# A new order of the small work around a 16-head attention tile: one head swapped between VectorE and GpSimd, two rows read from SBUF, casts and sums at other places

## The chip, the cores and the metric

One core of a Trainium2 chip. The metric is the device time of the whole program in microseconds. Engines are named TensorE (PE in the rows), VectorE (DVE), ScalarE (ACT), GpSimd (POOL) and SyncE (SP, which here only issues DMAs).

## The reference

Four layers on an input of 8 sequences of 1024 tokens with 256 channels, in float32: attention, a linear layer with fp8 rounding, a state-space mixer with its MLP, and a gated MLP, each with a layer norm ahead and a residual. The change touches the attention alone:

```python
q = (x @ Wq.T + bq).reshape(b, s, 16, 16)          # x is the layer norm of the input
attn_scores = einsum('bihd,bjhd->bhij', q, k) / 4
logits = li[:, :, None, :] + lj[:, None, :, :] + rel_b      # li, lj: three numbers per token
relation_probs = softmax(logits, axis=-1)                   # b, i, j, 3
bias = einsum('bijk,hk->bhij', relation_probs, logical_bias)
attn_scores = attn_scores + gate * bias                     # gate: sigmoid, per head and query
out = einsum('bhij,bjhd->bihd', softmax(attn_scores), v)
```

For each query i and key j there is thus a softmax over three relations, shared by all 16 heads, and each head adds its own mixture of it to its scores.

## The kernel before

The attention stage goes over 64 tiles of 128 queries, 8 tiles per sequence (called a batch here). For a tile there are two smooth terms, `R[k][0]` and `R[k][1]` (128 queries x 1024 keys, float32, in SBUF; k is the parity of the tile). Each head h does, in this order:

* f(h): `row = R1 * rho[h] + R0`. VectorE does it in one instruction (`dve_f`, L306), reading R1 from a copy in PSUM, `ps_p`, which ScalarE makes once a tile (`act_p`, L357). For the heads of `POOL_HEADS` GpSimd does it in two (`pool_f`, L224 and L226), from SBUF. Rows go through 8 buffers.
* TensorE computes the scores of head h into `ps_s` (`pe_s`, L465). There is one such buffer, so that of h+1 waits for s(h).
* s(h): VectorE adds the scores and the row, with a minimum along the keys (`dve_s`, L317).
* e(h): ScalarE takes the exponential (`act_e`, L394). Two heads later TensorE transposes (`pe_t`, L476), and ScalarE copies the two halves back (`act_at`, L403); TensorE then multiplies by V (L488).

While the heads of tile t run, four more jobs are done between them, at places written out by hand: `body` of each engine has a loop over u = 0..15 with lines such as `if look and u == 8: act_y0(act, t + 1)`; GpSimd's `body` is a plain list. Nothing is planned at run time: each engine goes through its own list in order, and semaphores make it wait.

1. The smooth terms of tile t+1. VectorE: two maxima into RT (`dve_rel`, L289 and L292, at u = 0 and 1). GpSimd: two subtractions (`pool_rel`, L199). ScalarE: three exponentials (`act_rel`, L377 and L381). GpSimd: two sums (`pool_sum`, L204 and L207). ScalarE: `act_y0`, an Ln (L387) and an Exp (L389). GpSimd: a product (`pool_t`, L211). VectorE: `dve_y` (L297, at u = 11, behind s(11)). GpSimd: two products (`pool_p`, L216), which end R0 and R1. They read a small tile `cur` (gate and two offsets per query), which ScalarE copies from `small` (`act_cur`, L352).
2. The projections of tile t+9: layer norm (`dve_ln` L248 at u = 2, `pool_rstd` L185, `dve_xn` L256 at u = 5), transposes and products on TensorE (`pe_xT`, `pe_d`, `pe_g`, `pe_qk_proj`), `act_d` (L340, L343), a clamp on GpSimd (`pool_gT`, L230), and q and k into `qkf` (`dve_qk`, L263 and L265, behind s(15)).
3. The splitting of that `qkf` into three bfloat16 parts, one tile later: `act_hi` (L362), `pool_rem` (L189), `act_mid` (L366), `pool_lo` (L193). The SP queue then writes the parts to HBM (`sp_parts`, L527), and reads them back as Q (L544, once a tile) and K (L536, once a batch, 24 DMAs in four groups; each group waits until the one before has landed and until the heads that use it are done in the last tile of the old batch). The order of this queue at a batch's end is: parts of the last tile of the next batch, 24 key loads, the loop's branch, the load of `xt` for the next layer norm (L522).
4. The output of tile t-1: `dve_norm`, `dve_out`, `act_o`, `act_aT`, `pool_xrb` (L243), and TensorE's transposes and product.

## Time and profile before

| | us |
|---|---|
| median of 3 runs | 6644.66 (6643.51 to 6645.17) |
| the profiled execution: its own time | 6645.17 |
| the profiled execution: its span | 6643.4 |
| attention stage, first to last tile | about 186 to 3153 |
| DVE busy in the span | 4750.4 (72%) |
| ACT busy | 4472.4 (67%) |
| PE busy | 5605.6 (84%) |
| POOL busy | 3670.1 (55%) |

The busy shares are means over stages of different kinds and cover the three later layers too. In the attention stage all four engines are busy most of the time and hand rows to each other head by head, so that a share alone doesn't say who waits. The order in time of one tile, engine by engine, does.

### The profile page before, as it was taken

What the parts mean: (1) busy time and instruction counts of PE and PEld (TensorE: products, weight loads), DVE (VectorE), ACT (ScalarE), POOL (GpSimd) and SP (SyncE); (2) the same over time, 40 slices, a digit from 0 to 9 for tenths busy, and PEclk for the clock granted to TensorE, in tenths of its full rate; (3) what the DMA queues carried; (4) which work ended last, traced back from release to release, by engine and by line L of the source; (5) the groups of instructions that cost most, each with busy time, mean ns of one, the idle gap of its engine ahead of it and who ended that gap; (6) DMA issues with size and microseconds to landing.
All of it is one profiled execution on the core that took longest, in us unless ns stands there. A gap on an engine that the chain in (4) does not pass through costs nothing. (4 is left out here: it accounts for less than half of the span.)

```text
span 6643.4 us, 125291 instructions
## 1 busy us (share of the span) xinstructions
PE 5605.6 (84%) x40354; PEld 3636.9 (55%) x40354; DVE 4750.4 (72%) x6130; ACT 4472.4 (67%) x7170; POOL 3670.1 (55%) x2047
## 2 busy tenths in 40 slices
PE   4688888888888888888436989889989988999999
PEld 3466666666565656655323444444444445666665
DVE  1788888888888888888776988888888792122121
ACT  1798989989898989999214778788787781111111
POOL 2777777777777777777122765675576580000000
PEclk7899999999999999999767989999999999999999
DMA  1212121111212121120222232232232222111110
GB/s 32 45 26 47 26 46 26 34 39 27 46 26 46 27 46 29 27 39 14 68 99 91 105 111 95 97 120 96 104 108 100 93 99 94 47 32 32 47 32 10
DMA packets 374621, 386.46 MB, mean 58 GB/s; under 512 B 223392, under 2 KB 300960, under 8 KB 374064
## 3 DMA queue, kind: packets, MB, share of 16 engines
q1 hardware_dynamic: 374064, 379.00, 19.8%
q8 instruction: 353, 5.78, 0.4%
q14 instruction: 204, 1.67, 0.1%
HBM read 293.58 MB, written 85.33 MB: 57 GB/s over the span
## 5 line engine op out<-in xcount | busy, mean ns | idle before, releaser
L317 DVE CUSTOM_DVE_ANT_0 srow<-srow,ps_s,cur 128x1024 f32<-128x1024 f32 x1024 | 1303.7, 1273 | 263.8 <-PE ps_s L465 183.0
L394 ACT ACTIVATE srow<-srow,nmax 128x1024 f32<-128x1024 f32 x1024 | 1190.9, 1163 | 207.8 <-DVE nmax L317 194.7
L403 ACT COPY AT<-ps_t 128x512 f32<-128x512 f32 x2048 | 1106.4, 597 | 73.5 <-PE ps_t L476 66.1
L1520 POOL TENSOR_TENSOR c_hc<-c_hs,c_cs 128x1024 f32<-128x1024 f32 x384 | 923.2, 2424 | 365.4 <-PE c_ps_y L1473 219.4
L476 PEld LDWEIGHTS ps_t<-ident,srow 128*128 128x128 f32 x8192 | 964.8, 143 | 279.7 <-ACT AT L403 84.8
L476 PE MATMUL ps_t<-ident,srow 128*128 128x128 f32 x8192 | 1106.0, 279 | 12.6 <-ACT AT L403 8.3
L1473 PE MATMUL c_ps_y<-c_hc,c_ident 128*128 128x512 f32 x2048 | 1009.0, 621 | 62.7 <-POOL c_hc L1520 61.9
L465 PE MATMUL ps_s<-K,Q 96*128 96x512 bf16 x2048 | 633.3, 391 | 436.9 <-DVE nmax L317 331.6
L306 DVE SCALAR_TENSOR_TENSOR srow<-ps_p,rho,R 128x1024 f32<-128x1024 f32 x768 | 975.0, 1270 | 13.7 <-ACT ps_p L357 9.2
L1784 DVE TENSOR_TENSOR_SCAN c_hs<-c_da,c_pd 128x1024 f32<-128x1024 f32 x384 | 868.6, 2279 | 151.7 <-PE c_pd L1459 128.4
L1570 ACT ACTIVATE c_sT<-c_room,c_bT 128x256 f32<-128x256 f32 x1536 | 647.8, 493 | 1.4
L226 POOL TENSOR_TENSOR srow<-srow,R 128x1024 f32<-128x1024 f32 x256 | 610.2, 2384 | 47.0 <-POOL srow L224 47.0
L488 PE MATMUL ps_o<-AT,V 128*32 128x128 f32 x16384 | 621.2, 281 | 1.6 <-issue 1.6
L1473 PEld LDWEIGHTS c_ps_y<-c_hc,c_ident 128*128 128x128 f32 x2048 | 367.0, 197 | 405.9 <-issue 288.5
L1459 PEld LDWEIGHTS c_pd<-c_ident,c_sT 128*128 128x128 f32 x3072 | 369.6, 147 | 319.7 <-issue 223.7
L1937 POOL TENSOR_TENSOR d_rstd<-d_ve,d_mhalf 128x4 f32<-128x4 f32 x16 | 16.3, 1019 | 898.6 <-DVE d_ve L969 898.6
L1512 POOL TENSOR_TENSOR c_db<-c_conv,c_bs 128x1024 f32<-128x1024 f32 x128 | 317.3, 2485 | 326.4 <-DMA c_bs<-bc_rows_d 225.2
L465 PEld LDWEIGHTS ps_s<-K,Q 96*128 96x128 bf16 x2048 | 133.4, 98 | 656.7 <-DVE nmax L317 542.7
L1561 ACT ACTIVATE c_da<-c_dt,c_a_neg 128x1024 f32<-128x1024 f32 x384 | 436.7, 1140 | 78.0 <-DVE c_hs L1784 77.7
L1459 PE MATMUL c_pd<-c_ident,c_sT 128*128 128x128 f32 x3072 | 422.2, 283 | 76.5 <-ACT c_sT L1570 60.9
L488 PEld LDWEIGHTS ps_o<-AT,V 128*32 128x32 f32 x16384 | 409.0, 111 | 137.3 <-issue 133.9
L199 POOL TENSOR_TENSOR R<-Dj,RT 128x1024 f32<-128x1024 f32 x128 | 300.8, 2372 | 301.9 <-DVE RT L292 301.9
(200 smaller groups left out, 8567.4 us busy)
## 6 DMA issues: line engine op xcount, KB each, us to landing
c_cs<-bc_rows_d SPq DMA_DIRECT2D x256, 512.0 KB, 3.8
c_bs<-bc_rows_d SPq DMA_DIRECT2D x64, 512.0 KB, 4.7
parts_d<-parts SPq DMA_DIRECT2D x65, 384.0 KB, 3.3
K<-parts_d SPq DMA_DIRECT2D x192, 128.0 KB, 4.5
Q<-parts_d SPq DMA_DIRECT2D x384, 64.0 KB, 2.9
ym_d<-c_conv SPq DMA_DIRECT2D x32, 512.0 KB, 2.6
d_ym<-ym_d SPq DMA_DIRECT2D x16, 1024.0 KB, 7.2
xt<-in_x SPq DMA_DIRECT2D x65, 128.0 KB, 3.3
```

The lines of the kernel that those rows point to most:

```text
L306: nc.vector.scalar_tensor_tensor(r[:], ps_p[:], rho[:, h:h + 1], R[k][0][:], ALU.mult, ALU.add).then_inc(fd_ok, 1)
L317: nc.vector.tensor_tensor_reduce(r[:], r[:], ps_s[:], cur[k][:, h:h + 1], BIG, ALU.add, ALU.min, nmax[:, h % NROW:h % NROW + 1]).then_inc( ...
L394: nc.scalar.activation(r[:], r[:], ACT.Exp, scale=-1.0, bias=nmax[:, h % NROW:h % NROW + 1]).then_inc(e_ok, 1)
L403: nc.scalar.copy(AT[h % NAT][:, HG * half:HG * half + HG, :], ps_t[:, half]).then_inc(at_ok, 1)
L465: last = nc.tensor.matmul(ps_s[:, n * 512:(n + 1) * 512], Q6[k][:, h, :], K6[:, h, n * 512:(n + 1) * 512], start=True, stop=True)
L476: last = nc.tensor.transpose(ps_t[:, half, i, :], rows_sb[h % NROW][:, j * P:(j + 1) * P], ident[:])
L488: last = nc.tensor.matmul(ps_o[32 * i:32 * i + 32, j, :], V[par][:, n, h, :], AT[h % NAT][:, n, :], start=(n == 0), stop=(n == NT - 1))
L1459: last = nc.tensor.transpose(pd[:, c, k * P:(k + 1) * P], src[:, k, c * P:(c + 1) * P], ident[:])
L1473: last = nc.tensor.matmul(ps_y[:, c, cut], ident[:], hc[(2 * n + c) % RING][:, cut], start=n == 0, stop=n == NS - 1)
L1520: nc.gpsimd.tensor_tensor(hc[(2 * n + c) % RING][:], hs[(2 * ROWS_T.index(n) + c) % NHS][:], cs[n % RING][:], ALU.mult).then_inc(hp_ok, 1)
L1570: last = nc.scalar.activation(sT[i % NSC][:, k, :], dtxT[:, k, pair * PD:(pair + 1) * PD], ACT.Copy, scale=bT[:, k, n:n + 1])
L1784: nc.vector.tensor_tensor_scan(hs[j % NHS][:], da[c][:], pd[:, c, :], 0.0, ALU.mult, ALU.add).then_inc(h_ok, 1)
```

## The change

* `POOL_HEADS` goes from (1, 4, 8, 12) to (4, 8, 12, 15). GpSimd no longer makes row 1 of the next tile ahead; it makes row 15 of the tile itself, behind the clamp.
* VectorE makes rows 0 and 1 from `R[k][1]` in SBUF in place of `ps_p` (`FROM_PSUM = 2`). Row 0 of the next tile comes ahead of s(15), row 1 behind it.
* The copy into `cur` goes from ScalarE to VectorE, ahead of L289, as a `tensor_scalar` with a wait for its own end.
* GpSimd's list: the remainder L189 comes ahead of the two subtractions, L193 ahead of f(8) and the sums.
* ScalarE's list: the second and third exponentials at u = 4 and 5 (they were at 3 and 4), L366 at 3 (4), `act_y0` at 9 (8), `act_d` at 11 (12), the copy into `ps_p` at 15 (14).
* TensorE's list: `pe_g` at u = 10 (11), `pe_qk_proj` at 12 and 13 (13 and 14).

```diff
--- before.py
+++ after.py
@@ -52,9 +52,10 @@
 
     AHEAD = NT + 1
     NROW = 8
-    POOL_HEADS = (1, 4, 8, 12)
+    POOL_HEADS = (4, 8, 12, 15)
     DVE_HEADS = tuple(h for h in range(H) if h not in POOL_HEADS)
     NPH, NDH = len(POOL_HEADS), len(DVE_HEADS)
+    FROM_PSUM = 2
     LAG = 2
     TINY, HUGE = 1e-15, 1e15
     NAT = 2 * HG
@@ -283,8 +284,13 @@
             d10, d20 = (Dj[:, i:i + 1, bass.ds(((t // NT) % 2) * S, S)].rearrange("p a s -> p (a s)") for i in range(2))
             a10, a20 = (cur[k][:, H + i:H + i + 1] for i in range(2))
             if step == 0:
-                wait(dve, cur_ok, t + 1)
+                wait(dve, kap_ok, t + 1)
+                wait(dve, a12_ok, t + 1)
                 wait(dve, p_ok, 2 * t)
+                wait(dve, s_ok, H * (t - 1))
+                nc.vector.tensor_scalar(cur[k][:].unsqueeze(1), small[:, bass.ds(t % (2 * NT), 1), :],
+                                        1.0, None, ALU.mult).then_inc(cur_ok, 1)
+                dve.wait_ge(cur_ok, t + 1)
                 wait(dve, pm_free, 4 * (NT * (t // NT) + NT) - 1)
                 nc.vector.tensor_scalar(RT[:], d10, a10, 0.0, ALU.add, ALU.max).then_inc(rel_step, 1)
             elif step == 1:
@@ -301,9 +307,12 @@
                 return
             r = rows_sb[h % NROW]
             if h == 0:
+                wait(dve, p_ok, 2 * t + 2)
+            elif h == FROM_PSUM:
                 wait(dve, pc_ok, t + 1)
+            p1 = R[k][1] if h < FROM_PSUM else ps_p
             wait(dve, t_ok, 2 * (H * t + h) + 2)
-            nc.vector.scalar_tensor_tensor(r[:], ps_p[:], rho[:, h:h + 1], R[k][0][:],
+            nc.vector.scalar_tensor_tensor(r[:], p1[:], rho[:, h:h + 1], R[k][0][:],
                                            ALU.mult, ALU.add).then_inc(fd_ok, 1)
 
         def dve_s(dve, t, k, h):
@@ -345,11 +354,6 @@
             last.then_inc(eT_ok, 1)
             act.wait_ge(eT_ok, p + 1)
             act.sem_inc(pm_free, 1)
-
-        def act_cur(act, t, k):
-            wait(act, kap_ok, t + 1)
-            wait(act, a12_ok, t + 1)
-            nc.scalar.copy(cur[k][:].unsqueeze(1), small[:, bass.ds(t % (2 * NT), 1), :]).then_inc(cur_ok, 1)
 
         def act_p(act, t, k):
             wait(act, p_ok, 2 * t + 2)
@@ -668,21 +672,20 @@
                 pool_t(pool, 0)
                 pool_p(pool, 0, 0, 0)
                 pool_p(pool, 0, 0, 1)
-                pool_f(pool, 0, 0, 1)
 
             def body(pool, t, k, par, ib, pro, post, look, before):
                 pool_f(pool, t, k, 4)
+                if followed(t, pro):
+                    pool_rem(pool, t - 1 + AHEAD)
                 for n in range(2 * look):
                     pool_rel(pool, t + 1, 1 - k, n)
                 if pro:
                     pool_rstd(pool, t + AHEAD)
                 if followed(t, pro):
-                    pool_rem(pool, t - 1 + AHEAD)
+                    pool_lo(pool, t - 1 + AHEAD)
                 pool_f(pool, t, k, 8)
                 for n in range(2 * look):
                     pool_sum(pool, t + 1, 1 - k, n)
-                if followed(t, pro):
-                    pool_lo(pool, t - 1 + AHEAD)
                 if post:
                     pool_xrb(pool, t - 1)
                 pool_f(pool, t, k, 12)
@@ -694,8 +697,7 @@
                     pool_p(pool, t + 1, 1 - k, n)
                 if pro:
                     pool_gT(pool, t + AHEAD)
-                if look:
-                    pool_f(pool, t + 1, 1 - k, 1)
+                pool_f(pool, t, k, 15)
                 if pro:
                     pool_kappa(pool, t + NT, 1 - par, ib)
 
@@ -732,6 +734,8 @@
                 for u in range(H):
                     if u + 1 < H:
                         dve_f(dve, t, k, u + 1)
+                    elif look:
+                        dve_f(dve, t + 1, 1 - k, 0)
                     dve_s(dve, t, k, u)
                     if look and u < 2:
                         dve_rel(dve, t + 1, 1 - k, u)
@@ -751,8 +755,6 @@
                         dve_gate(dve, t + NT)
                     if pro and u == 15:
                         dve_qk(dve, t + AHEAD)
-                    if look and u == 15:
-                        dve_f(dve, t + 1, 1 - k, 0)
 
             def finish(dve):
                 dve_out(dve, TILES - 2)
@@ -824,8 +826,6 @@
 
             def start(act):
                 front(act, NT)
-                for t in range(2):
-                    act_cur(act, t, t)
                 for step in range(3):
                     act_rel(act, 0, 0, step)
                 act_y0(act, 0)
@@ -842,9 +842,9 @@
                         act_hi(act, t - 1 + AHEAD)
                     if u == 0 and (not isinstance(t, int) or t >= 2):
                         act_aT(act, t - 2)
-                    if look and u in (1, 3, 4):
-                        act_rel(act, t + 1, 1 - k, (1, 3, 4).index(u))
-                    if followed(t, pro) and u == 4:
+                    if look and u in (1, 4, 5):
+                        act_rel(act, t + 1, 1 - k, (1, 4, 5).index(u))
+                    if followed(t, pro) and u == 3:
                         act_mid(act, t - 1 + AHEAD)
                     if post and u == 5:
                         act_o(act, t - 1)
@@ -852,14 +852,12 @@
                         act_gate(act, t + NT, 1 - par, ib)
                     if pro and u == 8:
                         act_xT(act, t + AHEAD)
-                    if look and u == 8:
+                    if look and u == 9:
                         act_y0(act, t + 1)
-                    if pro and u == 12:
+                    if pro and u == 11:
                         act_d(act, t + AHEAD)
-                    if look and u == 14:
+                    if look and u == 15:
                         act_p(act, t + 1, 1 - k)
-                    if u == 15 and not (isinstance(t, int) and t >= TILES - 2):
-                        act_cur(act, t + 2, k)
 
             def finish(act):
                 for u in range(H - LAG, H):
@@ -926,10 +924,10 @@
                         pe_xT(pe, p, om_next)
                     if pro and u == 9:
                         pe_d(pe, p, om_next)
-                    if pro and u == 11:
+                    if pro and u == 10:
                         pe_g(pe)
-                    if pro and u in (13, 14):
-                        pe_qk_proj(pe, p, om_next, u - 13)
+                    if pro and u in (12, 13):
+                        pe_qk_proj(pe, p, om_next, u - 12)
                     if post and u == 15:
                         pe_aT(pe, o, 4 * p + 3 if pro else last_p)
 
```

## Rows read from the trace of the kernel before

**Rows 1.** The copy of R1 into `ps_p`, one line of the program, whole trace.

```profile
L357 ACT COPY ps_p<-R x64: 1016/1036/1036, 211.3 to 3141.9; 128x1024 f32<-128x1024 f32 x64
```

**Rows 2.** Stretches of time from copy to copy: length, then busy time by engine.

```profile
1569.97:1615.02 45.05, 39.84 (x466) 28.84 (x466) 40.91 (x62) 42.42 (x66) 35.46 (x23) 1.00 0.12 28
1615.02:1661.77 46.75, 41.31 (x467) 30.16 (x466) 40.64 (x62) 42.28 (x66) 35.48 (x23) 0.96 0.12 27
...
1706.83:1763.45 56.62, 41.97 (x466) 30.36 (x466) 40.80 (x62) 42.72 (x66) 35.49 (x23) 0.88 0.36 57
2924.48:2967.27 42.79, 35.09 (x426) 24.11 (x426) 37.97 (x50) 40.26 (x58) 31.12 (x17) 1.00 0.07 17
```

**Rows 3.** Timeline of DVE, clean tile: start, duration, instruction, [idle before it].

```profile
1577.15 1.28 DVE L292 SCALAR_TENSOR_TENSOR RT<-Dj,cur,RT 128x1024 f32<-128x1024 f32 x1
...
1597.64 1.27 DVE L317 CUSTOM_DVE_ANT_0 srow<-srow,ps_s,cur 128x1024 f32<-128x1024 f32 x1
...
1602.74 1.28 DVE L317 CUSTOM_DVE_ANT_0 srow<-srow,ps_s,cur 128x1024 f32<-128x1024 f32 x1 [1.43 <-PE ps_s L465]
...
1603.95 1.22 DVE L297 SCALAR_TENSOR_TENSOR R<-RT,R 128x1024 f32<-128x1024 f32 x1
...
1613.78 1.28 DVE L317 CUSTOM_DVE_ANT_0 srow<-srow,ps_s,cur 128x1024 f32<-128x1024 f32 x1 [1.35 <-PE ps_s L465]
...
1617.82 1.28 DVE L317 CUSTOM_DVE_ANT_0 srow<-srow,ps_s,cur 128x1024 f32<-128x1024 f32 x1 [0.29 <-DVE srow L306]
```

**Rows 4.** Timeline of POOL in the same tile.

```profile
1594.51 1.18 POOL L193 TENSOR_TENSOR parts<-qkf,parts 128x512 bf16<-128x512 f32 x1
...
1601.24 2.38 POOL L211 TENSOR_TENSOR RT<-RT,R 128x1024 f32<-128x1024 f32 x1 [0.93 <-ACT R L389]
1605.35 4.72 POOL L216 TENSOR_TENSOR R<-R,R 128x1024 f32<-128x1024 f32 x2 [1.73 <-DVE R L297]
1610.78 1.07 POOL L230 TENSOR_SCALAR eT<-eT 128x256 f32<-128x256 f32 x1 [0.71 <-ACT eT L343]
1611.82 1.12 POOL L224 TENSOR_SCALAR srow<-R,rho 128x1024 f32<-128x1024 f32 x1
...
1615.48 0.22 POOL L238 TENSOR_TENSOR small<-cn,gate 128x16 f32 x1
```

**Rows 5.** Timeline of ACT in the same tile.

```profile
1576.14 0.63 ACT L362 CAST parts<-qkf 128x512 bf16<-128x512 f32 x1
...
1585.25 1.16 ACT L381 ACTIVATE R<-R,cur 128x1024 f32<-128x1024 f32 x1
...
1598.89 1.08 ACT L387 ACTIVATE R<-RT 128x1024 f32<-128x1024 f32 x1
1600.00 1.06 ACT L389 ACTIVATE R<-R 128x1024 f32<-128x1024 f32 x1
1600.96 1.13 ACT L394 ACTIVATE srow<-srow,nmax 128x1024 f32<-128x1024 f32 x1
...
1602.95 1.16 ACT L394 ACTIVATE srow<-srow,nmax 128x1024 f32<-128x1024 f32 x1
```

**Rows 6.** Waits of DVE in the attention stage: total, times, longest.

```profile
DVE stats L248 <- DMA xt<-in_x: 53.5, 6, 9.9
```

**Rows 7.** Timeline of the SP queue at a batch's end.

```profile
1311.22 0.41 SPq L527 DMA_DIRECT2D parts_d<-parts  x1
...
1350.10 0.35 SPq L522 DMA_DIRECT2D xt<-in_x  x1
```

**Rows 8.** Timeline of POOL, then of DVE, in the first tile.

```profile
216.99 2.36 POOL L226 TENSOR_TENSOR srow<-srow,R 128x1024 f32<-128x1024 f32 x1 [0.18 <-POOL srow L224]
...
218.13 2.30 DVE L292 SCALAR_TENSOR_TENSOR RT<-Dj,cur,RT 128x1024 f32<-128x1024 f32 x1
```

**Rows 9.** Lines L289 and L256: duration in ns, minimum, median, maximum.

```profile
L289 DVE TENSOR_SCALAR RT<-Dj,cur x64: 747/882/1735, 186.4 to 3103.0; 128x1024 f32 x51, 128x1024 f32<-128x1024 f32 x13
...
L256 DVE TENSOR_SCALAR xn<-xt,mv,rstd x65: 404/767/1090, 36.3 to 2811.2; 128x256 f32<-128x256 f32 x65
```

## The prediction

> **What bounds the kernel now.** Only the attention stage is touched, so I first looked for its beat: the 64 copies of the smooth term into PSUM, one per tile of queries, start from 211.3 to 3141.9 us [rows 1]. A table of stretches from copy to copy gives the periods. In the batch from 1388.03 to 1763.45 us five of eight take 45.05 to 45.07 us ("clean"), two some 46.8 us (a loop is gone round), one takes 56.62 us (a new batch begins) [rows 2]; the last batch, without projections, runs at 42.8 us. Over the 63 periods I count 36 clean, 14 with a loop-back, 6 at a batch's start and 7 of the last batch. In a clean period VectorE is busy 40.9 us, ScalarE 42.4, TensorE 39.8, GpSimd 35.5: no share names a bound, so I read one period in order of time.
>
> VectorE runs nearly without a gap [rows 3]. Name its instructions by head: f(h) builds the row, s(h) adds the scores. From the end of s(9) at 1598.84 to the start of y (L297) at 1603.95 are 5.11 us; from y to s(15) 9.83; from s(15) to the next tile's s(0) 4.04. Its gaps (1.43 and 1.35 us) are waits for the single score buffer where no f lies between two s. y waits for GpSimd's product L211, which ran 1601.24 to 1603.62 [rows 4], and that for ScalarE's Ln and Exp at 1598.89 and 1600.00 [rows 5]. So y has only 0.33 us to spare. This is what the reader should see: the chain Ln, Exp, product, y, products, f is already just in time.
>
> The other thing is the batch's start. Six times VectorE waits for the DMA of xt, 53.5 us in all, at most 9.9 [rows 6]. The queue shows why: the parts of a tile are written at 1311.22, the 24 key loads follow behind it, each group waiting for the last to land, and the load of xt is issued behind them, at 1350.10 [rows 7]. What starts this chain is the subtraction L193, at 1594.51 in the clean tile [rows 4].
>
> **Part by part.**
>
> *Parts earlier.* L193 now stands before f(8) and the sums, and its cast takes the place in ScalarE's order where the Exp L381 started at 1585.25 [rows 5]. Cast 0.63 us and 0.18 us of semaphore: L193 starts at 1586.06 instead of 1594.51, 8.45 us earlier. At a batch's start xt comes earlier by as much, and VectorE comes later by what is found below (over 3 us): 11.5 us are more than the 9.9 of the longest wait. All six waits go: **-53.5 us**. The queue's other conditions (keys overwritten only after heads 3, 7, 11 and 15 are done) aren't late by this shift.
>
> *y later.* Ln moves from behind e(8) to behind e(9) and its copies. e(9) can't start before s(9) ends: 1598.84, then 0.12 to ScalarE (as from s(12) to e(12)), 1.99 for e and its two copies (1600.96 to 1602.95 [rows 5]), 1.11 to Exp, 1.24 from Exp's start to the product's, 2.38 product, 0.15 to VectorE: 1605.83 against 1603.95. **+1.9 us** in every period, whatever room ScalarE has, since the chain starts at s(9). Behind y wait f(13), s(12), and the score buffer for TensorE. I take the same for the last batch.
>
> *f(15) by GpSimd.* It comes behind y, two products and the clamp of eT. Row by row, from y's start: products at 1.40 (1603.95 to 1605.35), 2.33 each, clamp at 6.06, 1.04 long (1610.78 to 1611.82), f(15) 3.66 (1611.82 to 1615.48): done at 10.76 [rows 4]. s(15) started 9.83 behind y, so it is late by at least 0.9. What VectorE saves is no time: its own f(15) is replaced by f(0) of the next tile at the same place, and the gap before s(15) only moves to s(14).
>
> *f(0) and f(1) from SBUF.* They no longer read ps_p, and both tensors now come from SBUF while GpSimd is in f(15) or f(4). Such an instruction is L292. It takes 1.27 us with GpSimd idle, but at 218.13 it took 2.30: L226 ran from 216.99 to 219.35, and L292 ended 1.08 behind that [rows 8]. So it waits for GpSimd's instruction to end, then needs some 1.0 us. The Trainium skill has this as a rule ("SBUF — State Buffer", Who interferes with whom): a DVE instruction with two SBUF inputs contends with a GpSimd instruction that reads SBUF, under an exclusive lock. It speaks against this edit, and this row agrees. By the rows: f(0) is issued 7.5 to 8.7 us behind y, inside f(15)'s pair (7.10 to 10.76). It runs behind it: s(15) at 11.76, **+1.9** against 9.83; if it slips in between the pair's halves, GpSimd is put off by 1.0 and s(15) comes at the same time. Then s(15) 1.2, qkf 0.86, f(1) issued at 13.8; GpSimd, free at 11.8, does kappa 0.2 and f(4) until 15.7; f(1) runs behind it and s(0) starts at 16.7: 4.9 behind s(15) instead of 4.04, **+0.9**. With a loop-back TensorE's restart holds s(1) anyway, and this is covered. In the last batch there is no clamp (1.0 less: +0.9 up to s(15)) and no qkf: f(1) is issued 1.2 behind s(15), when f(4)'s first half is about to end. I take it to get in before the second and to give back 0.8, since it neither waits for ps_p nor sits right before the s that needs it (if not, it costs some 2 more).
>
> *Remainder first on GpSimd.* The hi cast ends at 1576.77, so L189 (as large as L193, 1.18 us) would run to about 1578.1; L292 is at 1577.15 in the clean tile [rows 3, 5]. By the same lock it ends 0.8 late: **+0.8**, none with a loop-back, where L292 comes later than the cast. On the other side xn (L256), which is blocked in most tiles (0.77 us in the median, 0.40 at least [rows 9]), falls between GpSimd's instructions: **-0.4** in clean ones.
>
> *cur on VectorE.* The trace has no such copy there. The bounds are nothing and the 1.09 of xn's longest, which is larger and was blocked [rows 9]. I take 0.3, being nearer to a small step than to a blocked one. It is paid by L289, which runs into the end of f(4) (0.88 in the median, 0.75 at least [rows 9]) and won't any more: **0**, and up to 0.8 a period at the upper bound. ScalarE's 0.24 us less is off the path. Moving TensorE's projections one head earlier costs nothing: they must only be done before the clamp and qkf.
>
> Sum: clean 1.9+1.9+0.9+0.8-0.4 = 5.1, times 36 = 184; loop-back and batch start 1.9+1.9 = 3.8, times 20 = 76; last batch 1.9+0.9-0.8 = 2.0, times 7 = 14. With -53.5 that is +221 us. The profiled execution took 6645.2 us (span 6643.4), 0.5 over the median of 6644.66: about **6866 us**, 3.3% slower.
>
> **Rivals.**
> *No lock for f(0) and f(1).* One row carries it in this stage. Without it s(15) is late by 1.1 (10.9, with the semaphore), f(1) falls between and s(0) follows s(15) after 3.25, 0.8 sooner; L292 isn't held. Clean 1.9+1.1-0.8-0.4 = 1.8, loop-back 3.0, last batch 1.2: 65+60+8-53.5 = +80, 6725 us.
> *xn loses the lock.* From s(3)'s end xn is issued 5.12 us later (the addition 0.34, two f and two s of 1.195). On the other side stand 0.12 to e(3), 2.06 for it and its copies, the cast 0.63, 0.18, L193 1.13 and f(8)'s first half 1.13: that half ends at 5.25, the second starts 0.18 later. If VectorE is 0.3 later than I think, xn waits for the whole second half, 2.5 us more. In all 56 tiles that is +140: 7006 us. In one kind of period alone, 6916 (20 times) or 6956 (36 times).
> *Faster.* ScalarE and GpSimd could prove early enough, if s(9) is done 1.9 us sooner relative to y, or if the sums' new place frees ScalarE: then y keeps its place, f(15) too, and f(1) saves the wait for ps_p and the dependence of s(0) on the f just before it (0.8), xn 0.4: 36 times 1.2, and -53.5: -97, 6548 us. It decides at a chain from s(9) to y of 5.1 us; the rows make it 7.0. That it turns out so needs an instruction much shorter than its row.
> *No effect.* The gains at the six batch starts and the lateness could cancel at 1 us per period. Nothing in the rows makes that sum.
>
> **How the numbers follow.** Forecast with the lock 0.55 (6866), no lock 0.13, xn late in one kind of period 0.11, in all 0.09, faster 0.10, within 0.2% (13 us, about what a measurement can tell here) 0.02. The range is taken from 6720, just under the case without a lock, to 6985, over the partial xn case: it leaves out the full one and the faster side, 0.2. Within the forecast the last batch's f(1) is worth some 15 us and cur up to 50 upward. Faster 0.10, same 0.02, slower 0.88.
>
> **What would show it.** L248's six waits for xt gone; a wait of y for L211 of near 2 us in every tile; L306 with two SBUF inputs at 2 to 3 us in the mean for f(0) and f(1), not 1.27; clean periods of 50.1 us and loop-back ones of 50.6; in the last batch 44.8. Wrong it would be made by clean periods under 47 us: then y isn't late or the lock isn't met. Periods over 52 us mean that xn or something else is caught behind GpSimd.

## The result, and the profile after

| | before | after |
|---|---|---|
| median, us | 6644.77 | 6914.83 (6910.79 to 6922.61, 4 runs) |
| ratio | | 1.0408, 95% interval 1.0391 to 1.0426 |
| profiled execution, its own time | 6645.17 | 6920.26 |
| its span | 6643.4 | 6918.5 |

The change costs 270 us (275 between the two profiled executions). 221 were forecast, and the range of 6720 to 6985 holds the result.

First the stretches from copy to copy of `ps_p` in the kernel after, as in [rows 2]: length, busy time by engine, TensorE's granted clock, share and rate of DMA. The first is a batch's start, the second a period in which TensorE's clock falls (below), the third a clean one, the fourth one with a loop-back, and the fifth lies in the last batch.

```profile
1433.87:1486.96 53.09, 41.01 (x475) 30.23 (x464) 43.84 (x62) 42.47 (x66) 37.16 (x23) 0.94 0.20 43
1486.96:1539.32 52.36, 42.60 (x474) 31.11 (x464) 42.77 (x63) 42.87 (x65) 34.73 (x23) 0.93 0.09 22
1539.32:1589.68 50.36, 41.02 (x475) 30.10 (x464) 43.36 (x61) 42.99 (x65) 38.20 (x23) 0.97 0.11 27
...
1641.18:1691.78 50.60, 40.98 (x474) 30.22 (x464) 43.98 (x62) 42.45 (x65) 36.51 (x23) 0.97 0.11 25
...
3224.46:3271.97 47.51, 36.06 (x436) 25.31 (x426) 39.81 (x52) 40.47 (x58) 31.86 (x17) 0.96 0.07 16
```

The clean stretch is 50.36 us (50.1 forecast) and that with the loop-back 50.60 (50.6 forecast); the batch's start lost its long stretch (53.09 against 56.62); the one in the last batch (44.8 forecast) came out 2.7 us longer than forecast. But a single stretch misleads here: the copy now starts 1.5 us ahead of s(0) in some tiles and 0.1 behind it in others, and from s(0) to s(0) the tile of the third stretch takes 51.97 us. The means over all periods of a kind, from s(0) to s(0), worked out from the starts of s in both traces, in us (the forecast column is the mean before with the prediction's terms added):

| kind of period | before | forecast | after |
|---|---|---|---|
| clean (36) | 45.23 | 50.33 | 51.21 |
| loop-back (14) | 47.52 | 51.32 | 51.07 |
| batch's start (6) | 55.59 | 50.47 | 51.72 |
| last batch (7) | 43.39 | 45.39 | 48.02 |

The 54 us that the forecast lacks are thus 32 in the clean periods, 18 in the last batch and 8 at the batches' starts, with 4 the other way in the loop-back periods.

In the third stretch VectorE is busy 2.5 us more than in a clean one of before and GpSimd 2.7, TensorE 1.2 and ScalarE 0.6; the stretch is 5.3 longer, so much of it is waiting or standing still. The waits of VectorE in the attention stage say where (total us, times, longest):

```profile
DVE srow L326 <- PE ps_s L469: 272.5, 188, 4.3
DVE R L303 <- POOL RT L212: 130.2, 64, 16.6
...
DVE V L272 <- PE ps_m L457: 35.6, 55, 1.0
DVE RT L295 <- DVE cur L291: 19.3, 51, 0.4
DVE rinv L332 <- PE ps_m L502: 13.0, 59, 0.7
```

y (now L303) waits for the product in all 64 tiles. The wait for `xt` [rows 6] is gone. Then one clean tile in order of time, that of the third stretch above. GpSimd's second half of row 4 at its start:

```profile
1538.14 3.37 POOL L227 TENSOR_TENSOR srow<-srow,R 128x1024 f32<-128x1024 f32 x1 [0.18 <-POOL srow L225]
```

VectorE in this tile:

```profile
1537.99 1.28 DVE L315 SCALAR_TENSOR_TENSOR srow<-R,rho,R 128x1024 f32<-128x1024 f32 x1
...
1540.39 1.15 DVE L291 TENSOR_SCALAR cur<-small 128x18 f32 x1
1541.92 0.75 DVE L295 TENSOR_SCALAR RT<-Dj,cur 128x1024 f32 x1 [0.39 <-DVE cur L291]
...
1566.38 1.27 DVE L326 CUSTOM_DVE_ANT_0 srow<-srow,ps_s,cur 128x1024 f32<-128x1024 f32 x1
...
1574.49 1.23 DVE L303 SCALAR_TENSOR_TENSOR R<-RT,R 128x1024 f32<-128x1024 f32 x1 [1.73 <-POOL RT L212]
...
1582.16 1.28 DVE L326 CUSTOM_DVE_ANT_0 srow<-srow,ps_s,cur 128x1024 f32<-128x1024 f32 x1 [1.49 <-PE ps_s L469]
...
1583.36 3.02 DVE L315 SCALAR_TENSOR_TENSOR srow<-R,rho,R 128x1024 f32<-128x1024 f32 x1
1586.31 1.27 DVE L326 CUSTOM_DVE_ANT_0 srow<-srow,ps_s,cur 128x1024 f32<-128x1024 f32 x1
...
1588.37 2.87 DVE L315 SCALAR_TENSOR_TENSOR srow<-R,rho,R 128x1024 f32<-128x1024 f32 x1
1591.16 1.27 DVE L326 CUSTOM_DVE_ANT_0 srow<-srow,ps_s,cur 128x1024 f32<-128x1024 f32 x1
```

And GpSimd from the product on:

```profile
1572.10 2.37 POOL L212 TENSOR_TENSOR RT<-RT,R 128x1024 f32<-128x1024 f32 x1 [1.59 <-ACT R L393]
1575.90 4.71 POOL L217 TENSOR_TENSOR R<-R,R 128x1024 f32<-128x1024 f32 x2 [1.44 <-DVE R L303]
1580.57 1.08 POOL L231 TENSOR_SCALAR eT<-eT 128x256 f32<-128x256 f32 x1
1581.61 1.13 POOL L225 TENSOR_SCALAR srow<-R,rho 128x1024 f32<-128x1024 f32 x1
1582.93 2.38 POOL L227 TENSOR_TENSOR srow<-srow,R 128x1024 f32<-128x1024 f32 x1 [0.18 <-POOL srow L225]
1585.25 1.22 POOL L239 TENSOR_TENSOR small<-cn,gate 128x16 f32 x1
```

This is the forecast picture. y starts 1.73 us after VectorE is ready. Row 0 is issued at 1583.36, stands still while GpSimd's L227 runs to 1585.31, and needs 1.07 more; while it does so kappa (L239), 0.22 us long before [rows 4], takes 1.22. Row 1 at 1588.37 (2.87 us) meets row 4 of the next tile in the same way. This tile's own row 1, at 1537.99, came first: it took 1.28, and L227 at 1538.14, which took 3.37, stood behind it and held `cur` until 1541.54. s(15) starts 11.82 us behind y (11.76 forecast), the next s(0) 4.85 behind s(15) (4.9). Each of these blocked instructions follows the rule of the Trainium skill ("SBUF — State Buffer", Who interferes with whom) that the prediction weighed, and here the trace bears it out in both directions.

Over the whole stage the form with two SBUF inputs takes 2.1 us in the mean against 1.28 for the same instruction from PSUM. That mean covers two kinds of tile: in 29 of the 63 periods the two rows take some 3.0 and 2.9 us, in the other 27 of the first seven batches 1.3 to 1.6. By the groups of VectorE's instructions (busy us, mean ns):

```profile
L315 DVE SCALAR_TENSOR_TENSOR srow<-ps_p,rho,R 128x1024 f32<-128x1024 f32 x632 | 807.6, 1278 | 0.6 <-ACT ps_p L361 0.6
L315 DVE SCALAR_TENSOR_TENSOR srow<-R,rho,R 128x1024 f32<-128x1024 f32 x128 | 268.4, 2097 | 9.3 <-POOL R L217 4.8 <-issue 4.4
L298 DVE SCALAR_TENSOR_TENSOR RT<-Dj,cur,RT 128x1024 f32<-128x1024 f32 x63 | 89.9, 1426 | 0.0
...
L291 DVE TENSOR_SCALAR cur<-small 128x18 f32 x58 | 36.2, 624 | 0.0
```

**The same time cut at four points.** From the starts of s and y in all 64 tiles I worked out four distances, each a mean over the 63 periods, in us. The forecast column is the prediction's terms spread over the 63 periods.

| | before | forecast | after | parts early (b1) |
|---|---|---|---|---|
| s(9) to y | 6.28 | 8.18 | 8.13 | 6.28 |
| y to s(15) | 9.76 | 11.55 | 12.09 | 9.77 |
| s(15) to the next s(0) | 4.09 | 4.52 | 3.99 | 4.10 |
| s(0) to s(9) | 26.39 | 25.77 | 26.66 | 25.47 |
| period | 46.52 | 50.02 | 50.87 | 45.61 |

The first three rows together come out as forecast (24.21 us, 24.25 forecast). The shortfall of 0.85 us a period, 54 us in all, is that of the fourth, 0.89. But the two rows in the middle of the table agree only as a sum, and what lies behind that was not in the prediction. Of the 63 periods 28 take over 6.2 us from s(12) to s(14), most of them 6.8 to 8.3, while a tile such as the one above takes 5.32. TensorE's timeline in the tile before the one above shows why (start, duration; ps_s is the scores, L492 the product with V):

```profile
1522.38 0.86 PE L492 MATMUL ps_o<-AT,V 128*32 128x128 f32 x24
1526.01 1.03 PE L469 MATMUL ps_s<-K,Q 96*128 96x512 bf16 x2 [2.77 <-DVE nmax L326]
1526.84 1.91 PE L480 MATMUL ps_t<-ident,srow 128*128 128x128 f32 x8
1528.68 1.51 PE L492 MATMUL ps_o<-AT,V 128*32 128x128 f32 x24
1530.12 2.08 PE L435 MATMUL ps_m<-xnT,w_qk 128*128 128x128 f32 x8
...
1578.17 0.61 PE L469 MATMUL ps_s<-K,Q 96*128 96x512 bf16 x2 [2.76 <-DVE nmax L326]
1578.61 1.04 PE L480 MATMUL ps_t<-ident,srow 128*128 128x128 f32 x8
1579.58 0.86 PE L492 MATMUL ps_o<-AT,V 128*32 128x128 f32 x24
1580.37 1.16 PE L435 MATMUL ps_m<-xnT,w_qk 128*128 128x128 f32 x8
```

The late y leaves TensorE idle for 2.77 us. At 1526 it comes back slower: 1.91 us for transposes that take 1.04, 2.08 for a projection of 1.16. The granted clock of the stretch 1522 to 1532 is 0.68 of full in the mean, that of 1572 to 1583 is 1.00: the first stretch has part of its time at the lower of the two levels, 1.2 GHz. The same happens in six of the seven periods of the last batch, so that the clock falls at y in 33 of the 63. The scores of heads 13 and 14 come late, s(12) to s(14) takes 8.3 us and not 5.3. But by then GpSimd has made row 15 and is out of the way, so that rows 0 and 1 meet no lock, and s(15) to s(0) takes 3.25 us and not 4.85. The one loss replaces the other. A part is lost again right behind: `cur` takes 0.17 us where row 1 was held, and 1.15 where it was not, as at 1540.39, so that from s(15) to the next s(1) it is 7.85 us against 8.46.

The clock falls at a second place too, for which the prediction has no term: behind the pause that the new instructions ahead of s(1) leave TensorE at the start of a tile. In the tile after the one above:

```profile
1592.50 0.60 PE L469 MATMUL ps_s<-K,Q 96*128 96x512 bf16 x2 [2.21 <-DVE nmax L326]
...
1596.93 1.91 PE L480 MATMUL ps_t<-ident,srow 128*128 128x128 f32 x8
```

The trace has a stretch at the lower level there in 49 of the 64 tiles, that of b1 below (the parts early and nothing else) in 17. In clean periods s(2) to s(4) takes 5.50 us in the mean against 5.04 in b1, some 17 us in all. No run isolates this; where row 1 isn't held (x2) 19 tiles have such a stretch, and the distance is 5.11.

### The profile page after: what moved, and what is told of

It is laid out like the page before. It is cut to its first block and busy times, and to the rows that moved or that the text cites. A ratio compares the mean times of both kernels' runs of the same rounds, so it can differ in the third digit from the quotient of the medians.

```text
span 6918.5 us, 125391 instructions
## 1 busy us (share of the span) xinstructions
PE 5697.9 (82%) x40354; PEld 3722.8 (54%) x40354; DVE 4890.5 (71%) x6194; ACT 4500.0 (65%) x7106; POOL 3751.5 (54%) x2047
## 3 DMA queue, kind: packets, MB, share of 16 engines
q8 instruction: 353, 5.78, 0.4%
## 5 line engine op out<-in xcount | busy, mean ns | idle before, releaser
L326 DVE CUSTOM_DVE_ANT_0 srow<-srow,ps_s,cur 128x1024 f32<-128x1024 f32 x1024 | 1304.6, 1274 | 317.6 <-PE ps_s L469 272.5
L480 PE MATMUL ps_t<-ident,srow 128*128 128x128 f32 x8192 | 1135.9, 284 | 17.6 <-ACT AT L407 16.3
L480 PEld LDWEIGHTS ps_t<-ident,srow 128*128 128x128 f32 x8192 | 999.6, 146 | 278.1 <-ACT AT L407 68.2
L315 DVE SCALAR_TENSOR_TENSOR srow<-ps_p,rho,R 128x1024 f32<-128x1024 f32 x640 | 817.9, 1278 | 0.6 <-ACT ps_p L361 0.6
L227 POOL TENSOR_TENSOR srow<-srow,R 128x1024 f32<-128x1024 f32 x256 | 643.4, 2513 | 47.0 <-POOL srow L225 47.0
L492 PE MATMUL ps_o<-AT,V 128*32 128x128 f32 x16384 | 658.5, 294 | 0.3
L492 PEld LDWEIGHTS ps_o<-AT,V 128*32 128x32 f32 x16384 | 431.5, 115 | 148.8 <-issue 143.9
```

Source lines behind the costliest of these rows:

```text
L315: nc.vector.scalar_tensor_tensor(r[:], p1[:], rho[:, h:h + 1], R[k][0][:], ALU.mult, ALU.add).then_inc(fd_ok, 1)
L326: nc.vector.tensor_tensor_reduce(r[:], r[:], ps_s[:], cur[k][:, h:h + 1], BIG, ALU.add, ALU.min, nmax[:, h % NROW:h % NROW + 1]).then_inc( ...
L480: last = nc.tensor.transpose(ps_t[:, half, i, :], rows_sb[h % NROW][:, j * P:(j + 1) * P], ident[:])
L492: last = nc.tensor.matmul(ps_o[32 * i:32 * i + 32, j, :], V[par][:, n, h, :], AT[h % NAT][:, n, :], start=(n == 0), stop=(n == NT - 1))
```

## The experiments

Ratios are to the kernel before on the same chip. "x" kernels start from the changed kernel (6914.8 us, 1.0408), "b" kernels from the one before.

**x1, y back.** ScalarE's `act_y0` at u = 8 again; all else as changed.

```diff
-                    if look and u == 9:
+                    if look and u == 8:
                         act_y0(act, t + 1)
```

> The changed kernel with one edit undone: Ln and Exp of the next tile again behind e(8), not behind e(9). Theory (the chain from the end of s(9) is what makes y late): the wait of y for GpSimd's product falls from 130 us in all to under 15, a clean period from 50.4 to about 48.4, and TensorE, which no longer stands still for 2.7 us before s(12)'s scores, keeps its full clock for the projections behind: some 0.5 us more in the periods with a loop-back and in the last batch. 63 times 1.9 plus that: 6915 falls to about 6780, within 20. Rival (the sums of GpSimd, now behind f(8), are what is late, and Ln would wait for them at its old place too): the wait of y stays over 1 us and the time over 6850.

6807.06 us, ratio 1.0255 (1.0238 to 1.0272): 108 us off. s(9) to y falls from 8.13 to 6.47, the clock's dip at y is gone (s(12) to s(14) 5.23 in the mean, no period over 6), and VectorE waits for the product only ten times:

```profile
DVE R L303 <- POOL RT L212: 20.9, 10, 16.6
```

The rows stay locked, in every tile of the first seven batches now (2.82 us in the mean over all): s(15) to s(0) rises from 3.99 to 4.58. This is why the time is a little above what was expected: a part of what an earlier y gives goes back to the lock.

**b2, y late.** The reverse, on the kernel before: `act_y0` at u = 9 and nothing else.

> The kernel before with one part alone: Ln and Exp of the next tile behind e(9) and its copies, not behind e(8)'s. Theory (chain from the end of s(9), 7.0 us against 5.1): y starts 1.6 to 1.9 us later in every tile, 105 to 120 us in all; where TensorE, standing still meanwhile, is put to its lower clock, the projections behind it add to that, so 6640 rises to 6750 to 6790. Rival (y only takes over a gap of VectorE that comes later anyway, the one before s(15)): the gap before s(15) shrinks and the time stays under 6680.

6770.14 us, ratio 1.0190 (1.0159 to 1.0221): +130. The later y alone makes 1.85 us in 63 periods, 117 us, less the 19 that the waits for `xt` cover (53.5 to 34.1). Another 21 us are y to s(15), 9.76 to 10.09: in 15 of the periods, six of them in the last batch, TensorE's clock falls at y here too. The rest is not taken apart.

```profile
DVE R L297 <- POOL RT L211: 127.6, 64, 15.8
...
DVE stats L248 <- DMA xt<-in_x: 34.1, 6, 7.7
```

One line of ScalarE's order makes nearly half of the change's loss (130 us alone, 108 taken back, of 270).

**x2, rows 0 and 1 from PSUM.** The changed kernel, but rows 0 and 1 read `ps_p` as it stands, which is the copy of the tile before. This leaves out their right values; it keeps the same instructions at the same places, but ScalarE's copy now waits for row 1.

```diff
-            p1 = R[k][1] if h < FROM_PSUM else ps_p
+            p1 = R[k][1] if h < FROM_PSUM and isinstance(t, int) and t == 0 else ps_p
...
-            wait(act, fd_ok, NDH * t)
+            wait(act, fd_ok, NDH * t + FROM_PSUM)
```

> The changed kernel, but rows 0 and 1 are built from the copy in PSUM, as they stand in the list, so that they have one SBUF input. From the second tile on they so read the smooth term of the tile before, which leaves out their right values; ScalarE's copy into PSUM waits for row 1. Theory (VectorE's instruction with two SBUF inputs waits for GpSimd's running one): the two rows take 1.27 us instead of 2.10 in the mean; s(15) starts 10.9 us behind y instead of 11.8, since it waits only for row 15 itself, and s(0) 3.3 behind s(15) instead of 4.85. That is 2.5 us in a clean period and about 1 with a loop-back: 6915 falls to about 6805, within 25. Rival (the two rows are late because GpSimd's products or row buffers are, not for a lock): they'd start later or wait as before, and the time stays over 6880.

6844.84 us, ratio 1.0309 (1.0291 to 1.0326): 70 off, less than expected. That the lock is the cause of the long rows is shown: with one input in PSUM and GpSimd as busy as before they are back at 1.28 us, and s(15) to s(0) at 3.24. Rows 0 and 1 in one tile:

```profile
1601.11 1.28 DVE L315 SCALAR_TENSOR_TENSOR srow<-ps_p,rho,R 128x1024 f32<-128x1024 f32 x1
1602.88 1.28 DVE L326 CUSTOM_DVE_ANT_0 srow<-srow,ps_s,cur 128x1024 f32<-128x1024 f32 x1 [0.49 <-PE ps_s L469]
1604.94 1.28 DVE L315 SCALAR_TENSOR_TENSOR srow<-ps_p,rho,R 128x1024 f32<-128x1024 f32 x1
```

The gain is smaller than expected because the lower clock now stretches s(12) to s(14) in 38 of 63 periods (28 before the edit), and hides what s(15) would gain: y to s(15) only falls from 12.09 to 11.72.

**x4, row 1 ahead on GpSimd again.** `POOL_HEADS` is (1, 4, 8, 12): GpSimd makes the next tile's row 1 where it made row 15, VectorE makes row 15 from PSUM, and only row 0 is read from SBUF.

```diff
-    POOL_HEADS = (4, 8, 12, 15)
+    POOL_HEADS = (1, 4, 8, 12)
...
-                pool_f(pool, t, k, 15)
+                if look:
+                    pool_f(pool, t + 1, 1 - k, 1)
```

> The changed kernel with GpSimd's heads back at 1, 4, 8, 12 (row 1 of the next tile ahead, at the place of row 15); row 0 still comes from SBUF ahead of s(15). Theory: row 15 on VectorE falls into the gap of 1.5 us before s(14), so it costs nothing; row 0 still waits for the end of GpSimd's pair, so s(15) stays 11.8 us behind y; but row 1 isn't between s(15) and s(0), so s(0) starts 2.1 to 2.3 us behind s(15) instead of 4.85. Clean periods 2.4 us shorter, with a loop-back 1.3 (TensorE's restart then holds s(1)): 6915 falls to about 6795, within 25. Rival (the head on GpSimd is late because of the clamp and the products ahead of it, whatever head it is): s(1) waits for row 1, and the time stays over 6880.

6866.86 us, ratio 1.0337 (1.0320 to 1.0354): 48 off, where far more was expected. s(15) to s(0) falls to 2.25, but y to s(15) stays at 12.15, since 52 of 63 periods now have the stretched s(12) to s(14), and s(0) to s(1) grows from 4.17 to 5.05, since `cur` is caught behind row 4 each time:

```profile
L291 DVE TENSOR_SCALAR cur<-small 128x18 f32 x58 | 66.2, 1141 | 0.0
```

With y late, the place of row 15 is worth 48 us and not the 120 expected: what it gives at s(0) is in part taken by the clock and by `cur`.

**x5, TensorE kept busy in its pause.** In the changed kernel TensorE does head 9's transposes three times over; they stand ahead of the pause, and so fill part of the 2.77 us.

```diff
-                for i in range(HG):
+                for i in [i for _ in range(3 if h == 9 else 1) for i in range(HG)]:
```

> The changed kernel, in which TensorE transposes head 9 three times over, some 2 us more work in the time in which it has to wait for s(12) anyway; the results are the same. It tests what its idle time at y does. In the changed kernel s(12) to s(14) is 5.3 us in one kind of tile and 6.8 to 8.3 in another, in which the matmuls behind the pause run at half their speed. Theory (the pause brings the lower clock): with the pause filled s(12) to s(14) is 5.3 us in nearly all tiles of the first seven batches. The time itself hardly moves, 6915 within 20, since where s(14) is late row 0 comes behind GpSimd's instruction instead of waiting for it: s(15) to s(0) is then 3.25 us, not 4.85, so that the clock's loss is given back there. Rivals: the slow tiles come from loops and code loading, and stay; or the clock is a cost by itself, and 40 to 60 us are won.

6934.63 us, ratio 1.0440 (1.0411 to 1.0468): +20, which its interval doesn't tell from nothing. The dip at y is gone in all periods (s(12) to s(14) 5.23; VectorE waits 197.2 us for scores, not 272.5), and the time is not better: s(15) to s(0) is 4.58, the value with the lock in every tile. What s(12) to s(14) gains (6.25 - 5.23 = 1.02 us a period) is lost again from s(14) to s(15), where row 0 meets the lock (3.50 to 4.14), and from s(15) to s(0) (3.99 to 4.58). So the two do replace each other. The clock at the start of the tile isn't mended by this: 55 tiles have the lower level there.

**x3, `cur` back on ScalarE.** `act_cur` at u = 15 of ScalarE as before, ahead of L295 only the wait for it.

> The changed kernel with the copy into cur back on ScalarE, behind its copy into PSUM. The copy's 0.62 us in the mean and the 0.3 us wait behind it go. Theory (most of those 0.62 us are the wait for GpSimd's second half of row 4, which L295, the next instruction, would wait for just as well): only its own 0.2 us and the wait behind it are saved, 0.5 us in each period: 6915 falls by some 30, to 6885 within 12. Rival (all of it is saved): 0.9 to 1.0 us in each period, 6855.

6881.93 us, ratio 1.0362 (1.0344 to 1.0379): 33 off, as expected. The four distances put most of it where it should be: s(0) to s(9) falls from 26.66 to 26.17. Only half of that is `cur`'s own place, s(0) to s(1) (4.17 to 3.94); the other half is s(2) to s(4) (5.51 to 5.25), where the lower clock at the tile's start is now met in 30 tiles and not 49. And VectorE now waits for ScalarE's copy, 22.0 us in all.

**x8, exponentials back.** The second and third exponential of ScalarE at u = 3 and 4 again, behind the cast.

```diff
-                    if look and u in (1, 4, 5):
-                        act_rel(act, t + 1, 1 - k, (1, 4, 5).index(u))
                     if followed(t, pro) and u == 3:
                         act_mid(act, t - 1 + AHEAD)
+                    if look and u in (1, 3, 4):
+                        act_rel(act, t + 1, 1 - k, (1, 3, 4).index(u))
```

> The changed kernel with ScalarE's second and third exponentials at u = 3 and 4 again, behind the cast. Theory: from s(7) to s(9) the changed kernel is 0.26 us a period slower than the one before (5.72 against 5.46, in the last batch 6.15 against 5.54), since the third exponential at u = 5 stands ahead of the copy of O, and VectorE's reciprocal waits for TensorE's transposes of O (0.67 us in the last batch). If so, s(7) to s(9) comes to 5.46 to 5.50, in the last batch to 5.54, the waits of the reciprocal shrink from 13 us to under 4, and the time falls by 10 to 20 us to about 6900 us. Rival: the distance comes from y's later place (it stood in the experiments with y put back too, but not in the one with y alone made late), or from GpSimd's order; then nothing in it moves and the time stays at 6915 us.

6900.77 us, ratio 1.0381 (1.0364 to 1.0398): 14 off, less than can be told (the intervals overlap), but the distance is plain: s(7) to s(9) 5.49 us and not 5.72 (last batch 5.55 and not 6.15), and the reciprocal's wait is no longer among the seven longest. In the changed kernel the third exponential stands ahead of ScalarE's copy of `O`; in the last batch these two, TensorE's transposes of `O` and VectorE's wait follow each other directly. ScalarE:

```profile
3195.51 1.17 ACT L385 ACTIVATE R<-R,cur 128x1024 f32<-128x1024 f32 x1
3196.56 0.60 ACT L411 COPY O<-ps_o 128x512 f32<-128x512 f32 x1
```

TensorE:

```profile
3197.29 0.65 PE L502 MATMUL ps_m<-ident,O 128*128 128x128 f32 x4 [0.59 <-ACT O L411]
```

VectorE:

```profile
3197.98 0.26 DVE L332 RECIPROCAL rinv<-ps_m 128x16 f32<-128x16 f32 x1 [0.67 <-PE ps_m L502]
```

**b1, the parts earlier and nothing else.** The kernel before, with L193 ahead of f(8) and the cast at u = 3.

```diff
                     pool_rem(pool, t - 1 + AHEAD)
+                    pool_lo(pool, t - 1 + AHEAD)
                 pool_f(pool, t, k, 8)
...
-                if followed(t, pro):
-                    pool_lo(pool, t - 1 + AHEAD)
...
+                    if followed(t, pro) and u == 3:
+                        act_mid(act, t - 1 + AHEAD)
                     if look and u in (1, 3, 4):
                         act_rel(act, t + 1, 1 - k, (1, 3, 4).index(u))
-                    if followed(t, pro) and u == 4:
-                        act_mid(act, t - 1 + AHEAD)
```

> The kernel before with one part alone: the last part's subtraction directly behind the remainder, ahead of f(8), and its cast at u = 3 ahead of the second exponential; all else as it was. Theory (the batch's start waits for a chain of DMAs that begins with this subtraction): it starts some 8.4 us earlier, and the six waits for xt, 53.5 us in all, fall to under 6; GpSimd's sums come 1.3 us later, which they have room for. Some 0.4 us more may come in each tile from xn no longer meeting f(8)'s second half. 6640 falls by 45 to 70, to some 6585. Rival (the keys wait for the old batch's last heads, not for the parts): the waits stay over 30 us and the time over 6615.

6592.70 us, ratio 0.9927 (0.9901 to 0.9952), 48 us faster than before: the wait for `xt` is gone and this part of the change is good by itself. The clean periods stay at 45.21 us in the mean, from s(0) to s(0) (45.23 before): VectorE's xn is short now (0.41 us in the median, 0.79 before), but V waits for TensorE instead (35.1 us in all, 22.2 before):

```profile
DVE V L271 <- PE ps_m L453: 35.1, 55, 0.7
```

**b3 and b4, TensorE's order too.** From b1, with `act_y0` ahead of `act_xT` at u = 8 and `pe_d` at u = 10 (9), and in b3 also the first half of `pe_qk_proj` at u = 12 (13).

```diff
-                    if pro and u == 8:
-                        act_xT(act, t + AHEAD)
                     if look and u == 8:
                         act_y0(act, t + 1)
+                    if pro and u == 8:
+                        act_xT(act, t + AHEAD)
...
-                    if pro and u == 9:
+                    if pro and u == 10:
                         pe_d(pe, p, om_next)
```

> The kernel before with the parts early as in the run of that alone, and three places more: TensorE's first products of the projection at u = 10 (9), its last halves at 12 and 14 (13 and 14), and ScalarE's copy of the transposed tile behind Ln and Exp, not ahead. Theory: scores of head 11 no longer stand behind the products, so the gap before s(11) falls from 1.43 to 0.85 us, and y can follow since Ln starts 0.3 us earlier; the gap before s(15) falls by 0.3. Some 0.6 to 0.9 us in 56 tiles beyond the parts: 35 to 50 us, so 6640 falls to about 6540. Rival (y's chain takes over at once): no more than the parts alone give.

b3: 6630.26 us, ratio 0.9987 (0.9974 to 0.9999), 90 us short of what was expected. s(9) to y falls to 5.78 as meant, but s(12) to s(14) is 6.54. The projection at u = 12 waits in TensorE's list for `act_d`, which ScalarE does at the same u, and the scores stand behind it:

```profile
1558.49 1.16 PE L431 MATMUL ps_m<-xnT,w_qk 128*128 128x128 f32 x8 [0.78 <-ACTq L347]
1559.48 0.60 PE L465 MATMUL ps_s<-K,Q 96*128 96x512 bf16 x2
```

(The changed kernel has `act_d` at 11 with the projections at 12 and 13.) Without that last move:

> The kernel before with the parts early, ScalarE's copy of the transposed tile behind Ln and Exp, and TensorE's first products of the projection at u = 10 (9); its last halves stay at 13 and 14. Theory: in the run with the halves at 12 and 14 the half at 12 stood in TensorE's list ahead of the scores of head 14 and had to wait for ScalarE's copies at the same u, 1.9 us in each tile, which ate the 0.6 us won at y. With the halves back s(12) to s(14) is 5.1 us instead of 6.8, s(9) to y stays at 5.7, and the kernel is some 15 us faster than with the parts alone: 6578 within 15. Rival (the products at 10 are what delays): no faster than 6593.

b4: 6579.36 us, ratio 0.9908 (0.9891 to 0.9924). It is the fastest of all, though its interval overlaps that of b1, so that the second step isn't shown to be worth anything beyond the parts.

**x6 and x7, several back at once.** x6 is the changed kernel with y (x1), `cur` (x3) and the rows' source (x2) put back together; its rows 0 and 1 have not their right values either. In x7 L189 goes back behind the subtractions as well.

> The changed kernel with three edits undone at once: Ln and Exp behind e(8), rows 0 and 1 from the copy in PSUM (the term of the tile before from the second tile on, which leaves out their right values), cur on ScalarE. Singly they gave 108, 70 and 33 us. Theory (three delays in different places of VectorE's list, which add): 211 together, 6704 within 20. Rival (they overlap, since a wait for GpSimd that is cut in one place comes back in another): less than 170, over 6745.

> As the run with three edits undone, and GpSimd's remainder L190 again behind the reciprocal root, so that it doesn't stand ahead of the two subtractions. Theory (VectorE's second maximum, two SBUF inputs, is held by the remainder): the second maximum takes 1.27 us in every tile and 10 to 30 us are won over the run with three undone. What is left over the kernel before with the parts early (6593) is then the price of row 15 on GpSimd: s(15) 10.9 instead of 9.8 us behind y, 60 us less what its s(0) comes sooner. Rival (the remainder costs nothing): within 8 us of the run with three undone.

x6: 6680.55 us, ratio 1.0058 (1.0041 to 1.0075), 234 us off, more than was expected; the three alone gave 108 + 70 + 33 = 211. With y early no period has the clock's fall at y, and with the rows from PSUM no row is held, so neither loss can take the other's place. x7: 6675.12 us, 1.0051 (1.0032 to 1.0070), only some 5 us more, which can't be told from nothing, though L293 (before: L292) falls from 1481 to 1280 ns. In x6:

```profile
L293 DVE SCALAR_TENSOR_TENSOR RT<-Dj,cur,RT 128x1024 f32<-128x1024 f32 x63 | 93.3, 1481 | 0.0
```

In x7:

```profile
L293 DVE SCALAR_TENSOR_TENSOR RT<-Dj,cur,RT 128x1024 f32<-128x1024 f32 x63 | 80.7, 1280 | 0.0
```

x7 is still 82 us over b1. Row 15 on GpSimd, which s(15) waits for in all 63 periods, makes y to s(15) 1.22 us longer (10.99), but s(15) to s(0) 0.89 shorter (3.21): 21 us in all. The larger part is in s(0) to s(9), 26.31 against 25.47 or 53 us: ScalarE's exponentials (x8), and a wait for `cur`, which ScalarE copies right behind its copy into `ps_p`, now at u = 15 (14). GpSimd's kappa isn't what holds it: in one tile kappa starts at 1434.44, the copy into `ps_p` at 1438.16 and that into `cur` at 1439.11. The two waits of VectorE in x7:

```profile
DVE srow L321 <- POOL srow L227: 58.7, 63, 1.0
...
DVE RT L290 <- ACT cur L356: 35.1, 60, 1.9
```

## Why the prediction was nearly right, point by point

* *Parts earlier, -53.5.* Right. The waits for `xt` are gone; alone it gave -48 (b1).
* *y later, +1.9.* Right in place, size and cause: 8.13 - 6.28 = 1.85 in the mean of all periods, 130 us alone (b2), 108 taken back (x1). In the last batch it was mis-sized: 8.11 against 5.73 is 2.4, and not 1.9. The chain takes as long there as elsewhere, but VectorE had come to y sooner in the kernel before, and I took the clean tile's lateness.
* *f(15) by GpSimd and the lock of f(0).* Right in a tile with TensorE at full clock (11.82 against 11.76). In 28 of 63 periods the scores of heads 13 and 14 were late by 1.5 to 3 us, later than the row, which no step had. I looked at who waits for y on VectorE and GpSimd, and named TensorE's score buffer, but not that its pause slows the matmuls behind.
* *The lock of f(1), +0.9.* Right in those tiles (4.85 against 4.9), absent in 25 of the 28 (3.25). The mean of the two middle distances is therefore nearly as forecast, partly by luck: a loss without a term and a term that was met in only about half of the tiles.
* *L189 holds L292, +0.8.* Wrong in place. L298 is 1426 ns in the mean (+0.15): it takes 1.28 us where `cur` ahead of it was held, which delays it past the remainder, and in the other clean tiles 1.6 to 2.0. With `cur` away and y early it is 1481 (x6), and even that is 0.2 and not 0.8. Lifting it gave 5 us, which can't be told from nothing.
* *xn, -0.4.* The duration came as forecast, the gain did not: the wait moved to V, for TensorE (b1). The rival that xn is caught did not happen (0.41 in the median, 0.69 at most).
* *`cur`, 0.* This is the mis-sized term: 33 us (x3). Its 36.2 us busy and 19.3 of waiting for its own end are 0.9 a tile, against 0.1 got back from L289; part of it comes back in x3, as an L290 of 0.95 us and not 0.75 and as the wait for ScalarE's copy. I bounded it by xn's 1.09, took 0.3, and said that it is nearer to a small step than to a blocked one. It is both: 128x18 elements, and 1.15 us in the tile shown, behind GpSimd's row 4. By the Trainium skill ("VectorE: DVE Perf Modes", Mode 2×_2P) a single-source instruction between SBUF tensors can use both read ports. No run here tests the ports, but the trace agrees with an instruction that needs the lock, small as it is.
* *ScalarE's exponentials: no term.* 14 us (x8), by the copy of `O` behind them.
* *TensorE's clock at the tile's start: no term.* Some 17 us in the clean periods by the trace; a part of what `cur` gives back in x3 is this.
* *Loop-back periods: "TensorE's restart holds s(1) anyway".* Right. From s(15) to the next s(1) it was 7.99 to 8.66 us in the 14 such periods, 8.35 in the mean, and is 8.11 to 8.65, 8.46 in the mean: where the lock makes s(0) late, s(1) follows in 3.3 to 3.6 us, and where it doesn't, in 5.2 to 5.4. That rests on the trace alone; no run isolates it.

Of the 54 us that the forecast lacks, `cur` has 33 (with the part of the clock that goes with it) and the exponentials 14. The 7 left are a balance of xn's 14 (not realised), some 20 less for L292, and what is left of the lower clock at the tile's start; no run takes it apart. *No lock* falls by the rows of 3.02 and 2.87 us and by x2, *faster* by b2: y would have had to keep its place, and the move alone takes that away.

The sum is 221 against 275. Its parts were right where a row stood beside them. They failed where a step was carried over to another kind of period (the last batch, +4.6 us a period and not +2.0), where there was no row at all (`cur`), and where no term was thought of (TensorE's clock, the exponentials). That the whole came within 54 us owes something to losses that replaced each other.

## What to carry to other kernels

Follow a chain from the event that starts it to its consumer before moving one link of it: here one line of ScalarE's order made nearly half of the loss, and the change's one good part (the writes for the next batch earlier) was worth 48 us alone. When VectorE reads two tensors from SBUF, or is given even a small copy from SBUF to SBUF, look at what GpSimd runs at that moment; the same row read from PSUM took 1.28 us each time, and the same copy on ScalarE 0.2. Compare periods over all tiles, not one stretch, when the marker that cuts them has moved itself. And take losses apart in pairs: two of them (clock and lock) replaced each other, so that filling TensorE's pause gave nothing and freeing the rows gave 70 us where 110 were expected.

## What the runs showed of the hardware

* TensorE may lose half its clock after a pause of 2.77 us in an otherwise busy stage (1.91 us for 1.04, 2.08 for 1.16), for 3.4 or 6.8 us, and may not after one of 2.76 with the same instructions ahead of it. Pauses of 2.2 us at the tile's start, and in b2 nine of 1.7 us at y, were followed by the lower clock too. Filling the pause at y in part with transposes ended it there in all periods (x5). The Trainium skill ("TensorE: Matmul & The Clock Gate", Part 1) has the two levels, 1.2 and 2.4 GHz, set by how busy the engine has been; this agrees. What tells the two pauses apart stays open.
* The lock between VectorE and GpSimd works both ways, and takes in the smallest instructions: kappa 0.22 to 1.22 us (1.2 in 46 of 64 tiles), L227 2.38 to 3.37 behind row 1, `cur` 0.17 or 1.15.
